# A weight rounding moved from ScalarE to GpSimd in the eight-expert stage, with the order of two engines rewritten

## The reference

```
p      = softmax(xn @ Wr.T)                # 8 experts, xn = layer-normed x
top2   = the two best experts of each token, weights renormalised to 1
y_e(t) = silu(xn[t] @ W1[e].T) @ W2[e].T   # 256 -> 1024 -> 256
x[t]  += sum over the two chosen e of weight * y_e(t)
```

## Time and profile before

| | |
|---|---|
| median of three runs (lowest, highest) | 1704.21 us (1702.52, 1705.05) |
| the profiled execution, its own time | 1704.21 us |
| its span (first to last instruction) | 1702.4 us |
| PE busy | 1550.2 us, 91% |
| DVE busy | 1153.1 us, 68% |
| ACT busy | 813.4 us, 48% |
| POOL busy | 594.9 us, 35% |
| the 23 blocks of the changed stage | from about 627 us to 910 us of the span |

### The profile page before, as it was taken

How to read it: one execution, slowest core, us unless ns; L and a number is a source line. 1 busy time by engine, 2 the same in 40 slices (tenths; PEclk the granted TensorE clock), 3 DMA queues, 4 the chain that set the end, 5 groups by cost and what they waited for, 6 DMA issues and landing times. The chain is left out here.

```text
span 1702.4 us, 39132 instructions
## 1 busy us (share of the span) xinstructions
PE 1550.2 (91%) x15530; PEld 1204.2 (71%) x15530; DVE 1153.1 (68%) x2441; ACT 813.4 (48%) x1815; POOL 594.9 (35%) x501
## 2 busy tenths in 40 slices
PE   6988989999998899999999788888889788999998
PEld 3444467555576589999998555666678688599997
DVE  4576869982057456777762446888689777578887
ACT  1232752121134436666664327777637622566664
POOL 2330200000011047865633325677559653112210
PEclk8897999999989989999999899999989899999999
DMA  9993049621023467676745854766200010001001
GB/s 293 325 318 98 1 145 226 125 54 44 1 93 112 121 197 271 241 242 205 235 152 145 244 184 136 230 201 197 80 25 1 16 29 4 13 13 38 20 7 50
DMA packets 151364, 218.43 MB, mean 128 GB/s; under 512 B 38353, under 2 KB 124753, under 8 KB 145297
## 3 DMA queue, kind: packets, MB, share of 16 engines
q1 hardware_dynamic: 115008, 107.80, 22.6%
q0 software_dynamic: 10368, 58.47, 10.7%
q10 hardware_dynamic: 25808, 49.68, 9.0%
HBM read 168.85 MB, written 47.05 MB: 127 GB/s over the span
## 5 line engine op out<-in xcount | busy, mean ns | idle before, releaser
L321 PE MATMUL ps<-kv_ctx,kv_w 128*128 128x257 f32 x512 | 138.6, 407 | 18.9 <-PEq L1743 8.1
L2209 POOL TENSOR_TENSOR a_pr<-a_pr,a_inv 128x1028 f32<-128x1028 f32 x64 | 121.9, 1906 | 71.8 <-DVE a_inv L2321 71.4
L325 PE MATMUL ps<-kv_w,kv_ctx 128*128 128x256 f32 x512 | 131.6, 403 | 13.7 <-ACT kv_kv L345 13.7
L321 PEld LDWEIGHTS ps<-kv_ctx,kv_w 128*128 128x128 f32 x512 | 97.7, 203 | 41.1 <-issue 16.4
L325 PEld LDWEIGHTS ps<-kv_w,kv_ctx 128*128 128x128 f32 x512 | 99.8, 201 | 37.1 <-ACT kv_kv L345 22.0
L2297 ACT ACTIVATE a_pr<-ps,a_neg 128x257 f32<-128x257 f32 x256 | 117.8, 480 | 0.6 <-DVE a_neg L2340 0.6
L1556 POOL TENSOR_TENSOR b0m_pm<-b_dr,b_gates 128x256 f32<-128x256 f32 x16 | 13.2, 831 | 289.7 <-SPq L1520 260.8
L111 PE MATMUL ps<-f_xTH,f_w1H 128*128 128x256 f32 x368 | 106.7, 290 | 1.5 <-DVE f_xTL L1952 1.5
L2046 DVE TENSOR_TENSOR f_hL<-f_hr,f_hH 128x512 fp32r<-128x512 f32 x92 | 75.6, 847 | 45.3 <-ACT f_hH L1895 45.2
L3190 DVE SCALAR_TENSOR_TENSOR x<-ps,g_gate,x 128x256 f32<-128x256 f32 x256 | 105.2, 475 | 0.0
L112 PE MATMUL ps<-f_xTL,f_w1H 128*128 128x256 f32 x368 | 104.8, 285 | 0.0
(11 more groups left out here) (416 smaller groups left out, 4470.5 us busy)
## 6 DMA issues: line engine op xcount, KB each, us to landing
a_kv<-kv SPq DMA_DIRECT2D x64, 513.0 KB, 4.0
kv<-kv_kv ACTq DMA_DIRECT2D x53, 513.0 KB, 5.7
a_ctxT<-in_ctxT SPq DMA_DIRECT2D x32, 514.0 KB, 8.0
a_ctxR<-in_ctx SPq DMA_DIRECT2D x32, 512.0 KB
kv_ctx<-in_ctxT ACTq DMA_DIRECT2D x61, 257.0 KB, 3.3
outs<-f_yo SPq DMA_DIRECT2D x23, 256.0 KB, 2.6
a_vB<-vlast SPq DMA_DIRECT2D x16, 256.0 KB
kv<-f_kv ACTq DMA_DIRECT2D x5, 513.0 KB, 10.6
```

Source lines behind the costliest of these rows:

```text
L321: done = e.matmul(out[:, 0:NK], self.w[:, 0, c, cols(part)], ctx[:, c, :], start=(c == 0), stop=(c == DC - 1))
L325: done = e.matmul(out[:, cols(t, D)], ctx[:, c, cols(t)], self.w[:, 1, c, :], start=(c == 0), stop=(c == DC - 1))
L2209: e.tensor_tensor(pr[:, b % RP, :, :], pr[:, b % RP, :, :], inv[:, b % 2, :].unsqueeze(2).to_broadcast([P, HG, NK]), ALU.mult).then_inc(*p ...
```

## The change

`high2` moves from ACT's list to POOL's and becomes a `tensor_copy` there. On POOL the order within a turn becomes: rows, `gather2`, `gather1`, `high1`, `high2`; before it was rows, `high1`, `gather1`, `gather2`. On DVE `low1(j+1)` moves from before the four hL of block j to behind them. No buffer, no matmul and no DMA is added or removed.

```diff
-        p_hi1, a_hi2 = Y.sig("pool", "hi1"), Y.sig("act", "hi2")
+        p_hi1, p_hi2 = Y.sigs_of("pool", "hi1 hi2")
...
+                def high2(j):
+                    e.wait_ge(*ld_w2[j % 2].at(16 * (j // 2 + 1)))
+                    if j >= 2:
+                        e.wait_ge(*t_y.at(j - 1))
+                    e.tensor_copy(flat(w2[0], j), raw2[:, j % 2, :]).then_inc(*p_hi2.up())
...
                     if j + 2 < BLOCKS:
                         gather_rows(j + 2)
                     if j + 1 < BLOCKS:
-                        high1(j + 1)
+                        gather2(j + 1)
                     if j + 2 < BLOCKS:
                         gather1(j + 2)
                     if j + 1 < BLOCKS:
-                        gather2(j + 1)
+                        high1(j + 1)
+                    high2(j)
...
-                def high2(j):
-                    e.wait_ge(*ld_w2[j % 2].at(16 * (j // 2 + 1)))
-                    if j >= 2:
-                        e.wait_ge(*t_y.at(j - 1))
-                    e.activation(flat(w2[0], j), raw2[:, j % 2, :], ACT.Copy).then_inc(*a_hi2.up())
-
...
-                        high2(j)
...
                 def low2(j):
-                    e.wait_ge(*a_hi2.at(j + 1))
+                    e.wait_ge(*p_hi2.at(j + 1))
...
                     if j and j + 1 < BLOCKS:
                         turned(j + 1)
-                        low1(j + 1)
                     for q in range(4):
                         e.wait_ge(*a_h.at(4 * j + q + 1))
                         e.tensor_tensor(h[1][:, j % 2, 2 * q:2 * q + 2, :], hr[:, q, :, :], h[0][:, j % 2, 2 * q:2 * q + 2, :].bitcast(F32),
                                         ALU.subtract).then_inc(*v_l.up())
+                    if j + 1 < BLOCKS:
+                        low1(j + 1)
                     if j == 0:
-                        low1(1)
                         turned(1)
                     low2(j)
```

## The result

| | before | after |
|---|---|---|
| median, lowest to highest, 8 runs each on one chip | 1704.09 us (1694.28 to 1711.54) | 1718.24 us (1715.55 to 1725.71) |
| ratio with its 95% interval | | 1.0106 (1.0085 to 1.0127) |
| the profiled execution's own time, span | 1704.21, 1702.4 | 1719.8, 1717.8 |

The change makes the kernel 1.06% slower, 18 us by the ratio. The interval is 14.5 to 21.6 us of 1704.1. The forecast was 1724.3 us, 20.1 more than before, within 1709 to 1728. All ratios leave out a run over 1.5% above the fastest of its kernel; that is a single one, of 1746.07 us, in the kernel of the change with POOL's order undone.

What follows compares the result with a forecast made beforehand. The prediction took PE's own work, 11.95 us a turn, to bound the loop. 20 turns x 0.95 = 19.0 us plus 1.1 at the start made 20.1 on 1704.2, forecast 1724.3 us, range 1709 to 1728.

Steps and rivals of the forecast that it cites:

- What bounds it: Block loop: PE's own work, busy 24.00 of 24.00 us, 11.95 a turn; relieving ACT buys nothing, the change can only make PE wait.
- The chain to the copies: POOL, from the end of low2: wake 0.27, DMA 0.95, gap 0.30, DMA 0.95, so high1 starts 2.5 us after low2.
- The collision: POOL copies and DVE subtractions with both inputs in SBUF exclude each other, for 1.75 us (copy) and 0.55 us (hL).
- the 2.8 of the forecast: DVE in the loop: hL q0 was to show some 2.8 us in the changed profile.
- the prediction's own signs: Changed profile: wrong if PE has no waits for f_w1L, low1 starts before T+9, or an hL sits between no two copies.
- Who wins at the edge: POOL against DVE: q0 asks 0.4 us ahead of high1, inside the DMA before it, and the copy wins.
- the other outcome: Rival, 28%: q0 runs before high1, one hL fewer behind the copies; turn 12.45 us, time 1715.3 us.
- The turn: Block loop: low1 ends at T+12.8, next T at T+12.9, 0.95 us over 11.95; 20 turns give 19.0 us.
- The start: Block 0: high2(0) waits for its load until 636.7 and delays low1(1); PE starts block 1 1.1 us later.
- Nothing behind the loop gives it back: After the loop: PE is busy 17.90 of 18.00 us in its last stretch, and the following stage waits for the last block's output.
- The view named for it: PE's waits in the changed profile: L111 for DVE f_w1L, near 20 us in total over some 20 times.
- The rival that the cushion holds: Rival, 15%, not slower: DVE gets the port at each request, low1 ends at T+10.6, PE never waits; 1704.2 or 1705.3 us.

## Why the prediction was right

**What bounds it.** Right: PE's 11.95 was full, ACT's relief bought nothing (the orders alone, with ACT as before, gave the same time), and the only thing to watch was when low1 is done.

**The chain to the copies.** Right to 0.1 us: wake 0.27, DMA 0.94, gap 0.30, DMA 0.94. With T at 793.99 (a turn of 12.97 before 806.96) high1 starts at T+4.57, for 4.6; q0 asks at T+4.31, for 4.23.

**The collision.** Its size is right and its order is wrong. "The two copies do not run through without DVE" failed. They do run through: q0 waits for both, 4.56 us for the 2.8 of the forecast. By the prediction's own signs this counts against its mechanism: it called itself wrong if an hL sits between no two copies, and in 19 of the 20 turns none does. The row from which I had the opposite was the pair of POOL instructions in the earlier trace rows, the second of which has to wait for the first by a semaphore; there POOL stops. The kernels with a stop show that this matters. The sum was hardly touched, because DVE has four hL to run behind or between two copies in any order: the copies end at T+8.31 instead of 8.7, four hL follow instead of three, and low1 starts at T+10.60 for my 10.55. So the time came out right although the order did not, and that part is luck; with the stop ahead of the copies, where q0 goes before high1, the turn is 0.5 us shorter.

**Who wins at the edge.** Right, by the earlier trace rows: the DVE instruction that asked 0.26 us before the copy, inside the DMA ahead of it, waited. The prediction had q0 0.4 ahead, where its row had 0.32; that it would have lost there too is shown by the hL that asked 0.51 ahead in the kernel with POOL's order undone. The row cited for the other outcome (718.54) was said to be as deep in its DMA as q0; by the prediction's own times q0 would be 0.58 deep and not 0.44, and the 0.68 measured is further off still. What set it apart is that no copy followed its DMA. I gave 28% to the other outcome, and the stop shows that it was a real one. The rule of the Trainium skill, SBUF — State Buffer, section "Who interferes with whom", that whoever issues first has the pair of ports, would have q0 ahead of high1 in the changed kernel; at 798.30 it was not. The exclusive lock itself, in the same section, agrees with the rows: low1 that asked 0.10 us after a copy had begun took 3.96 us in place of 2.28.

**The turn.** Forecast 12.9, measured 12.97 with PE starting 0.10 after low1, as estimated. Of the 20 turns one has 12.48. There high1 waited 0.19 us for its load to land, so POOL had a stop by accident:

```profile
656.64 1.98 POOL L1762 CAST f_w1H<-f_raw 128x2048 fp32r<-128x2048 f32 x1 [0.19 <-DMA f_raw<-in_L_ffn_W1T,f_wrow]
658.57 2.35 POOL L1768 CAST f_w2H<-f_raw 128x2048 fp32r<-128x2048 f32 x1
```

Q0 ran in 0.69 there and the second copy took 2.35, the same picture as with the stop put in on purpose. The sum over the loop is 19.6 us for my 19.0.

**The start.** The 1.1 us can't be shown. The load of W2 was issued 2 us earlier in this run and took 9.6 us for 11.6, so that high2(0) began at 632.70, and low1(1) at 635.94, earlier than the 637.50 of the earlier trace rows; the clock was higher too. The term is lost in what differs from run to run.

**Nothing behind the loop gives it back.** Neither shown nor refuted. The loop alone is 19.6 us longer in the trace, the whole kernel 14.5 to 21.6 us by the interval, and the medians lie 14.2 apart. All of the loop's 19.6 may have come through, or some 5 us of it may have gone lost in waits behind it. The kernel with the stop ahead of the copies has 10.6 us more between its drains than before, and its ratio says 5.0 to 15.9. The kernel with half of high2 asks the same: 20 turns of 0.16 are 3.2 us, and the ratio says 1.2 to 10.4. I leave it open.

**The view named for it.** I had said that PE's waits would stand at DVE f_w1L. They stand at "issue", 20 of them, 15.1 us. The count was right and the name wrong; only the two timelines show the releaser. The view also counts less than the turns do: 15.1 us in place of the near 20 that I had named, while the 20 turns are together some 20 us longer.

**The rival that the cushion holds** fell. It was right that a single copy is about even: with the orders alone, one copy on POOL, the turn stays 11.95.

## What to carry to other kernels

An engine at half load is not a free place for work: what counts is whether the moved instruction shares a lock with something in the circle that sets the pace, and what it takes there then stands in the turn, here one for one. Before moving a copy to GpSimd, list the VectorE instructions with two SBUF inputs that can be asked for while it runs, and count the indirect-DMA issues beside them too. Where VectorE has short work that others need, it can pay to make GpSimd stop ahead of its copies by a real wait: here it took 0.5 us of 12.97 off a turn, which was still longer than the 11.95 of before, and a stop between the copies took off 0.13.

## What the runs showed of the hardware that I had not expected

- Two POOL copies right behind POOL's issue of an indirect DMA kept DVE's subtractions out from the first to the last (3.74 us), whether the subtraction asked 0.26 us before the first copy or 0.95 us inside it. A memset ahead of the copies or between them (0.04 us) did not open it.
- A memset with a wait for its signal (0.18 us) changed that: ahead of the copies q0 ran at once, between them one waiting hL got in. Where that stop, or a wait for a load, stood ahead of the first copy, an hL that asked inside it also got in between the two copies, with nothing between them.
- A DVE subtraction that asks during a DMA issue on POOL lost to a copy right behind that issue when it asked 0.26, 0.32 and 0.51 us ahead of the copy. At 0.90 us ahead it ran at once.
- The issue of an indirect DMA by POOL was held by a DVE subtraction that had begun 0.13 to 0.14 us before it: 3.00 us instead of 0.95, ending 0.84 to 0.85 after the subtraction.
- PE's wait for a DVE result can appear as "issue" in the profile.
